# Padding rows in front of each expert's rows, written at fixed places during the attention passes

## The chip, the cores and the metric

The kernel runs on one core of a Trainium2 chip. Five engines work side by side and meet in semaphores: TensorE (PE, with its weight loads PEld), VectorE (DVE), ScalarE (ACT), GpSimd (POOL) and SyncE (SP), which here issues most of the DMA transfers. SP, ACT and POOL each have a queue of their own for DMAs (SPq, ACTq, POOLq in the profile). The metric is the device time of one execution in microseconds, lower is better.

## What is computed

The input x is 8 sequences of 512 tokens with 256 numbers each, 4096 tokens in all. First comes a layer of linear attention with a decaying sum, then a layer of experts: 32 routed experts, of which every token takes the best 4, and one shared expert. Cut to what matters:

```python
x = x + attn(layernorm(x))                    # decaying running sums of k and k*v, 8 sequences
xf = layernorm(x)
top_vals, top_idx = top_k(xf @ router_w.T + router_b, 4)
rw = softmax(top_vals) * 1.8
g = silu(einsum('th,eih->tei', xf, gate_w)); u = einsum('th,eih->tei', xf, up_w)
routed = einsum('tei,ehi,te->th', g * u, down_w, one_hot(top_idx) weighted by rw)
shared = silu(xf @ sg.T) * (xf @ su.T) @ sd.T
out = x + routed + shared
```

## The kernel before

**Two halves.** The attention runs as nine passes of a software pipeline (`steps`, b = 0 to 8), one per sequence of 512 tokens (`TS` = 4 tiles of 128) with work of two earlier sequences folded in. Pass b does the projections of sequence b ("now"), the output projection, the second norm and the router of sequence b-1 ("before"), and the numbering of the routed rows of sequence b-2 ("past"). Beside them it turns three experts' weights into place (`prep`; they come by `load_experts`, lines 365 to 369, issued by SP at the end of the pass before). Then come 192 tiles of 128 rows through the experts: 32 tiles of the shared expert (t = 0 to 31, "the shared tiles") and 160 routed tiles (t = 32 to 191). The order on each engine is the order in which the code is written.

**The lists.** A routed tile holds rows of one expert only. So every token's row (1088 bytes: its numbers in two halves, its number, its four shares and experts) is written four times into a table in HBM, `xlist`, which has a stretch of `CAP` = 4224 rows for each expert. SP loads a tile of 128 rows from `xrow` into one of four buffers `list_row` (`load_list(j)`, line 441), and POOL scatters it four times by the row numbers in `dest` (`list_rows`, line 587; 32 tiles, 128 scatters). `load_list(j)` waits until the scatters of tile j-4 have landed, since it takes their buffer, and SP stands still in that wait. 80 of the 128 scatters lie in passes 3 to 8 (twelve in each of passes 3 to 7, twenty in pass 8, woven between POOL's other work by `list_some`), 48 behind them, beside the shared tiles.

**The padding.** An expert's last tile may reach past its last row. Rows with a token number of T (= 4096) and share 0 have to stand there; their results go to a dump. Before, this padding stands behind an expert's rows, where the count of the rows puts it. The counts are known only at t = 1 (`count_tiles`, lines 952 to 957). At t = 8 to 15 SP therefore reads four places at a time (line 498) and issues four stores of 128 rows each from `pad_row` (line 500), 32 in all, with one more at line 496.

**POOL beside it.** In each pass POOL also has the products of q with the running sums (line 567 and 571, two of each), two roots for the norms (lines 576 and 578; `root(0, b+1)` for the next sequence's first norm, `root(1, b-1)` for the second norm), the split of the second norm's result in two halves (line 627), and the numbers of the rows (line 594). PE's sums over the heads (`den`, line 1276) of pass b+1 wait for both products of line 567 of pass b. VectorE's reciprocal of them (lines 838 and 840) is first in VectorE's pass.

**The shared tiles.** For a tile PE turns the rows (line 1119), multiplies by gate and up (line 1147), turns the result (1167) and multiplies by down (1180). ScalarE takes the output to `y_sb`, four buffers (line 692, or 690 for routed tiles), and SP stores it (line 493). At t = 5, 8, ... 29 the last nine experts are brought in: SP loads one (line 399), ScalarE takes its high halves (lines 700 and 702), VectorE the low ones (1037, 1039). The routed tiles can only begin behind the last of them, and their first load waits on SP for all scatters and pads (line 412).

Of the kernel before, what the change touches and what calls it, by code (L numbers as in the profile page):

```python
# [5 lines left out]
def moe_block(nc, x, w_qkv, w_out, decay_param, router_w, router_b, gate_w, up_w, down_w,  # L6
# [6 lines left out]
    P = 128  # L13
# [34 lines left out]
    with ctx:  # L48
# [12 lines left out]
        xlist = nc.dram_tensor("xlist_scratch", [E * CAP + P, ROW // 2], f32, kind="Internal").ap()  # L61
# [3 lines left out]
        x1_v = acc[0][0:T].rearrange("(b j p) h -> b p j h", j=TS, p=P)  # L65
        acc1_tiles = acc[1][0:T].rearrange("(j p) h -> j p h", p=P)
# [55 lines left out]
        pad_i = carve(E)[0:1].bitcast(i32)  # L122
        counts, tiles, tile_end = carve(E), carve(E), carve(E)
        ended = [carve(E) for _ in range(2)]
        pad_row = carve(ROW // 2)
# [45 lines left out]
        list_row = [sb(f"list_row{n}", [P, ROW // 2], f32) for n in range(LISTS)]  # L171
        payload = sb("payload", [P, TS * (ROW // 2 - H)], f32)[:, :].rearrange("p (j w) -> p j w", j=TS)
# [81 lines left out]
        counts_ready, pads_ready, pads_listed = sem("counts_ready"), sem("pads_ready"), sem("pads_listed")  # L254
# [31 lines left out]
        def tiles_listed(b):  # L286

            return range(3 * (b - 3), 3 * (b - 2)) if 3 <= b < NB else range(3 * (NB - 3), 3 * (NB - 3) + 5) if b == NB else range(0)

        IN_WINDOW = tiles_listed(NB)[-1] + 1  # L290
# [93 lines left out]
        def _(sp):  # L384
            row_at = [[sp.alloc_register(f"row_at{half}_{n}") for n in range(BATCH)] for half in range(2)]
            pad_at = [sp.alloc_register(f"pad_at{n}") for n in range(4)]
            row_of = [0] * TILES

            def rows_of(batch):

                sp.load(row_at[batch % 2], row_i[0:1, BATCH * batch:BATCH * (batch + 1)])
                for n, r in enumerate(row_at[batch % 2]):
                    row_of[NT + BATCH * batch + n] = sp.snap(r, min_val=0, max_val=E * CAP)
# [7 lines left out]
            def load_tile(t):  # L401
# [7 lines left out]
                else:  # L409
                    if t == NT:  # L410
                        for j in range(NT - LISTS, NT):
                            sp.wait_ge(*listed(j))
                        sp.wait_ge(pads_listed, 16 * (E + 1))
# [29 lines left out]
            def step(st):  # L443
                b = st.b
                if b == 3:
                    load_list(0)
                if b >= 3:
                    for j in tiles_listed(b)[1:3]:
# [17 lines left out]
                if b >= 3:  # L466
                    for j in tiles_listed(b)[3:]:
                        load_list(j)
                    load_list(tiles_listed(b)[-1] + 1)
# [10 lines left out]
            for t in range(TILES + ROUND):  # L480
# [6 lines left out]
                if t % 5 in (0, 2):  # L487
                    j = IN_WINDOW + 1 + t // 5 * 2 + (t % 5) // 2
# [5 lines left out]
                if t == 8:  # L494
# [829 lines left out]
```

## Time and profile before

| | us |
|---|---|
| median of 3 runs | 765.24 (763.4 to 765.39) |
| the profiled execution | 765.09 |
| its span, first to last instruction | 763.1 |
| PE busy | 604.8 (79%) |
| VectorE busy | 525.8 (69%) |
| ScalarE busy | 421.5 (55%) |
| POOL busy | 468.3 (61%) |

The span is 2 us shorter than the profiled execution's time, which has the start and end around it. A busy time is a sum over stages: the attention passes fill the span up to 297 us, the shared tiles from there to about 400 us, and the routed tiles what follows, with the sums of the three accumulators as the last stretch. What a change is worth has to be read in the stage where it acts.

### The profile page before, as it was taken

To read this page: it belongs to the slowest core of one execution; us is meant where nothing else is said; L and a number is where in the kernel's file an instruction comes from. 1 tells how busy PE (TensorE), PEld (TensorE's weight loads), DVE (VectorE), ACT (ScalarE), POOL (GpSimd) and SP (SyncE) were. 2 spreads that over 40 slices of the span, in tenths; PEclk is the share of its full clock that TensorE was granted. 3 is DMA by queue.
4 is the path that set the end of the run, shared out by engine and by line. 5 is a ranking of instruction groups with operands and counts; after the bars stand their busy time and mean duration, and the time that the engine had idled before them with its cause. 6 is when DMAs were issued, how large, how long until landed. Compare 5 with 4: busy or idle time off the path is not lost.

```text
span 763.1 us, 15317 instructions
## 1 busy us (share of the span) xinstructions
PE 604.8 (79%) x4649; PEld 421.6 (55%) x4649; DVE 525.8 (69%) x1931; ACT 421.5 (55%) x1008; POOL 468.3 (61%) x401
## 2 busy tenths in 40 slices
PE   4888884868768764877779999999999999999200
PEld 2455553554546453554447777777777777777100
DVE  2798996989798875664546666666666666666163
ACT  1534534352525413564557788887888887888200
POOL 3142347766666757763625778788888878888500
PEclk9998997989799876998889999999999999999755
DMA  9556264656557356999946888888988888887699
GB/s 298 201 144 187 85 189 140 197 161 207 167 159 237 102 175 196 298 328 303 310 140 123 140 141 144 142 139 138 144 144 142 145 141 136 145 140 114 127 412 395
DMA packets 122738, 140.66 MB, mean 184 GB/s; under 512 B 22370, under 2 KB 112002, under 8 KB 122626
## 3 DMA queue, kind: packets, MB, share of 16 engines
q1 hardware_dynamic: 89952, 97.42, 41.9%
q0 software_dynamic: 29184, 38.82, 30.6%
q10 hardware_dynamic: 3522, 3.44, 1.3%
q8 instruction: 39, 0.64, 0.4%
q14 instruction: 41, 0.34, 0.2%
HBM read 74.88 MB, written 65.02 MB: 183 GB/s over the span
## 4 chain that ended last, share of the span: by engine, by line
PE 52%; DVE 23%; DMA 8%; ACT 5%; SPq 4%; issue 4%; POOL 3%; POOLq 0%; ACTq 0%; DVEq 0%
PE psD L1180 12%; PE psK L1147 11%; PE psQ L1147 11%; PE psT L1119 5%; DVE W L831 2%; DMA acc_scratch<-arena 2%; SPq L509 2%; DVE arena L804 2%; DMA W<-acc_scratch 2%; DVE stats L785 2%; PE psT L1167 2%; PE psV L1167 2%; POOL xlist_scratch L587 2%; PE psT L1079 1%; PE psT L1069 1%
## 5 line engine op out<-in xcount | busy, mean ns | idle before, releaser
L650 POOL DMA_INDIRECT acc_scratch<-arena x160 | 251.4, 1571 | 78.5 <-issue 30.9
L587 POOL DMA_INDIRECT xlist_scratch<-list_row,dest x128 | 130.5, 1020 | 71.3 <-DMA list_row<-xrow_scratch 35.4
L1180 PE MATMUL psD<-W,arena 128*128 (+1 forms) x960 | 138.8, 276 | 1.0 <-DVE arena L987 0.9
L991 DVE COPY arena<-psT 128x512 f16<-128x512 f16 x192 | 81.3, 424 | 77.4 <-PE psT L1119 74.3
L1147 PE MATMUL psQ<-W,arena 128*128 (+1 forms) x576 | 113.7, 335 | 14.4 <-DVE arena L991 14.2
L1147 PE MATMUL psK<-W,arena 128*128 (+1 forms) x576 | 112.4, 333 | 12.4 <-DVE arena L991 12.2
L1180 PEld LDWEIGHTS psD<-W,arena 128*128 128x128 f16 x960 | 86.9, 99 | 8.8 <-DVE arena L987 1.1
L681 ACT ACTIVATE arena<-arena 128x192 f16<-128x192 f32 x192 | 69.6, 363 | 30.9 <-DVE arena L1015 20.0
L1147 PEld LDWEIGHTS psQ<-W,arena 128*128 128x128 f16 x576 | 51.8, 100 | 50.7 <-DVE arena L991 16.0
L1021 DVE TENSOR_TENSOR arena<-arena 128x64 f16<-128x64 f32 x192 | 43.4, 226 | 50.5 <-ACT arena L681 50.5
L1147 PEld LDWEIGHTS psK<-W,arena 128*128 128x128 f16 x576 | 51.3, 99 | 47.9 <-DVE arena L991 14.5
L1119 PE MATMUL psT<-ident,arena 128*128 128x128 f16 x768 | 76.3, 223 | 0.8 <-issue 0.7
L1119 PEld LDWEIGHTS psT<-ident,arena 128*128 128x128 f16 x768 | 58.8, 100 | 31.7 <-issue 10.3
L690 ACT ACTIVATE arena<-psD,arena 128x256 f32<-128x256 f32 x160 | 73.3, 458 | 2.2 <-DMA acc_scratch<-arena 1.4
L1022 DVE TENSOR_TENSOR arena<-arena 128x128 f16<-128x128 f32 x192 | 54.6, 285 | 0.0
L831 DVE SCALAR_TENSOR_TENSOR W<-psT,W 128x384 f16<-128x384 f32 (+1 forms) x72 | 40.1, 589 | 19.8 <-ACT W L717 19.3
L678 ACT ACTIVATE arena<-psT 128x384 f16<-128x384 f16 x96 | 47.1, 490 | 10.0 <-PE psT L1167 5.9
L721 ACT ACTIVATE W<-psK 128x512 f32<-128x512 f32 x16 | 9.6, 597 | 76.2 <-PE psK L1191 76.2
L678 ACT ACTIVATE arena<-psV 128x384 f16<-128x384 f16 x96 | 47.1, 490 | 6.5 <-PE psV L1167 1.2
L717 ACT ACTIVATE W<-psT 128x384 f16<-128x384 f32 (+1 forms) x72 | 36.4, 528 | 20.2 <-PE psT L1084 10.3
L567 POOL TENSOR_TENSOR W<-W 128x512 f32<-128x512 f32 x16 | 20.4, 1272 | 43.2 <-DVE W L815 43.1
L674 ACT ACTIVATE arena<-psQ 128x192 f32<-128x192 f32 x96 | 31.6, 330 | 26.5 <-PE psQ L1147 26.4
(156 smaller groups left out, 1115.0 us busy)
## 6 DMA issues: line engine op xcount, KB each, us to landing
arena<-xlist_scratch SPq DMA_DIRECT2D x160, 136.0 KB
W<-acc_scratch SPq DMA_DIRECT2D x24, 512.0 KB, 12.6
acc_scratch<-arena SPq DMA_DIRECT2D x16, 512.0 KB, 4.8
arena<-in_w_late_dram SPq DMA_DIRECT2D x9, 640.0 KB, 4.9
arena<-in_L_attn_x_dram SPq DMA_DIRECT2D x10, 512.0 KB, 5.4
xlist_scratch<-arena SPq DMA_DIRECT2D x33, 136.0 KB
arena<-in_L_ffn_down_w_dram SPq DMA_DIRECT2D x23, 192.0 KB
list_row<-xrow_scratch SPq DMA_DIRECT2D x32, 136.0 KB, 5.0
```

What stands on the lines that cost most here:

```text
L587: nc.gpsimd.indirect_dma_start(xlist[:, :], bass.IndirectOffsetOnAxis(ap=dest[:, n:n + 1], axis=0), list_row[j % LISTS][:, :], None).then_ ...
L650: nc.gpsimd.indirect_dma_start(acc[t % ACCS][:, :], bass.IndirectOffsetOnAxis(ap=token[:, (t - NT) % DEEP:(t - NT) % DEEP + 1], axis=0), y ...
L678: nc.scalar.activation(aT[u].rearrange("p n t -> p (n t)"), psA[u], ACT.Copy).then_inc(aT_done, 1)
L681: nc.scalar.activation(halves[t % 2][:, 0:I], act32[t % 2], ACT.Copy).then_inc(a_hi_done, 1)
L690: nc.scalar.activation(y_sb[(t - 2) % ROUND], psY[t % 2], ACT.Copy, scale=share[:, (t - 2 - NT) % DEEP:(t - 2 - NT) % DEEP + 1]).then_inc( ...
L831: nc.vector.scalar_tensor_tensor(dst, bank_of("prep", n)[:, 0:width], WS, hi, ALU.mult, ALU.subtract).then_inc(prep_lo, 1)
L991: nc.vector.tensor_copy(xT[t % 2].rearrange("p s c t -> p (s c t)"), psX[t % 2]).then_inc(xT_done, 1)
L1021: nc.vector.tensor_tensor(both[:, I:2 * P], act32[t % 2][:, P:I], both[:, P:I], ALU.subtract).then_inc(a_split, 1)
L1022: nc.vector.tensor_tensor(both[:, 2 * P:3 * P], act32[t % 2][:, 0:P], both[:, 0:P], ALU.subtract).then_inc(a_split, 1)
L1119: last = nc.tensor.transpose(psX[t % 2][:, n * P:(n + 1) * P], xg[t % XG][:, n * P:(n + 1) * P], ident16[:, :])
L1147: last = nc.tensor.matmul(psG[t % 2][:, 0:GU], xT[t % 2][:, sx, h], weights(t, (2 * h + sw) * GU, GU), start=(n == 0), stop=(n == 3 * HC - 1))
L1180: last = nc.tensor.matmul(psY[u], aT[u][0:height, part], weights(t - 2, GUW + q * H, H, height), start=(n == 0), stop=(n == len(parts) - 1))
```

## The change

1. The padding of an expert stands in front of its rows, in the first 128 rows of its stretch, at a place that needs no count. POOL makes the padding rows once, in the set-up, in `list_row[0]`; SP stores them in pass 1 into a small block in HBM, `pad_scratch`, waits for that, and copies the block from HBM to HBM to 32 fixed places: 5, 5, 6, 5, 5 and 6 copies in passes 1 to 6, behind the load of the residual and ahead of the list loads and `load_experts`. The 33 stores at t = 8 to 15 and their eight reads of places are gone.
2. The real rows of an expert begin at row 128 of its stretch: `seen[0]` starts at 1 in each of 128 partitions in place of 0, so that the ranks start at 128. The tiles of an expert are laid so that the last ends at its last row, and the first reaches back into the padding. The arithmetic of `count_tiles`, `end_tiles`, `own_tiles` and `place_tiles` on VectorE changes with it: 17 small operations in place of 16.
3. The scatters are portioned anew: 4 in pass 2 (three of them ahead of that pass's second product of line 567, one behind line 571), 14 in each of passes 3 to 7, and 20 in pass 8. That makes 94, with 34 left beside the shared tiles. In passes 3 to 8 two scatters stand ahead of the split of line 627 where one stood. The list loads on SP move with them.

```diff
+        pad_block = nc.dram_tensor("pad_scratch", [P, ROW // 2], f32, kind="Internal").ap()
...
+        pad_row = list_row[0][:, :]
...
-        def tiles_listed(b):
...
+        LIST_FROM = [0, 0, 0] + [4 + 14 * n for n in range(NB - 2)] + [94]
+        FETCHED = [(LIST_FROM[b] + 7) // K for b in range(NB + 2)]
+        PADDED = [E * max(b - 1, 0) // (NB - 2) for b in range(NB + 1)]
...
+                if j == 0:
+                    sp.wait_ge(pad_stored, 16)
...
+                if b == 1:
+                    sp.wait_ge(pads_made, 1)
+                    sp.dma_start(pad_block, pad_row).then_inc(pad_stored, 16)
+                    sp.wait_ge(pad_stored, 16)
+                if 1 <= b < NB - 1:
+                    for e in range(PADDED[b], PADDED[b + 1]):
+                        sp.dma_start(xlist_e[e, 0:P], pad_block).then_inc(pads_listed, 16)
+                if b >= 2:
+                    for j in range(FETCHED[b] + 2 if b >= 3 else 0, FETCHED[b + 1]):
                         load_list(j)
...
-                if t == 8:
-                    sp.wait_ge(pads_ready, 2)
-                    sp.dma_start(xlist[E * CAP:E * CAP + P], pad_row).then_inc(pads_listed, 16)
-                if 8 <= t < 8 + E // 4:
-                    sp.load(pad_at, pad_i[0:1, 4 * (t - 8):4 * (t - 7)])
-                    for r in pad_at:
-                        sp.dma_start(xlist[bass.ds(sp.snap(r, min_val=0, max_val=E * CAP), P)], pad_row).then_inc(pads_listed, 16)
...
-            nc.gpsimd.memset(seen[0][:, :], 0.0).then_inc(route_made, 1)
+            nc.gpsimd.memset(seen[0][:, :], 1.0).then_inc(route_made, 1)
...
-                list_some(8, 9)
+                if b >= 3:
+                    list_some(8, 10)
                 if st.before:
...
-                list_some(9, 12)
+                list_some(10 if b >= 3 else 0, 13 if b >= 3 else 3)
                 if st.now:
                     k_sum_product(b, 1)
                     kv_sum_product(b, 1)
-                list_some(12, 20)
+                list_some(13 if b >= 3 else 3, 20)
```

POOL in pass 2, from its split (line 627) to the first root of pass 3. L567 and L571 (569 and 573 in the change) are the products, L594 (596) the row numbers, L576 and L578 (578 and 580) the root. Before:

```order
L627 TENSOR_TENSOR arena<-arena 128x2x256 x2
L567 TENSOR_TENSOR W<-W 128x512
L571 TENSOR_TENSOR W<-W 128x512
L594 IOTA payload 128x4
L587 DMA xlist_scratch<-list_row,dest 135296x272 x3
L576 TENSOR_TENSOR vare<-mv,eps 128x4
L578 TENSOR_TENSOR rstd<-vare,mhalf 128x4
```

And in the changed kernel:

```order
L627 TENSOR_TENSOR arena<-arena 128x2x256 x2
L589 DMA xlist_scratch<-list_row,dest 135168x272 x3
L569 TENSOR_TENSOR W<-W 128x512
L573 TENSOR_TENSOR W<-W 128x512
L589 DMA xlist_scratch<-list_row,dest 135168x272
L596 IOTA payload 128x4
L589 DMA xlist_scratch<-list_row,dest 135168x272 x3
L578 TENSOR_TENSOR vare<-mv,eps 128x4
L580 TENSOR_TENSOR rstd<-vare,mhalf 128x4
```

The first three scatters have moved ahead of pass 2's second pair of products, and one more lies behind it.

SP at the end of pass 2, between the payload's store and the experts' loads. The change puts five copies and two list loads ahead of L365. Before:

```order
L431 DMA xrow_scratch<-payload 128x4x16
L458 DMA acc_scratch<-arena 128x4x256
L460 DMA xrow_scratch<-arena 128x4x256
L465 DMA arena<-in_L_attn_x_dram 128x4x256
L365 DMA arena<-in_L_ffn_gate_w_dram 128x3x256
```

And in the changed kernel:

```order
L430 DMA xrow_scratch<-payload 128x4x16
L457 DMA acc_scratch<-arena 128x4x256
L459 DMA xrow_scratch<-arena 128x4x256
L464 DMA arena<-in_L_attn_x_dram 128x4x256
L471 DMA xlist_scratch<-pad_scratch 16x2176 x5
L442 DMA list_row<-xrow_scratch 128x272 x2
L365 DMA arena<-in_L_ffn_gate_w_dram 128x3x256
```

Passes 1 and 3 to 6 have the copies at the same place.

## Rows read from the trace of the kernel before

**Rows 1.** Timeline of ACT, late experts' first copies: start, us, engine, line, tiles

```profile
313.58 0.83 ACT L700 ACTIVATE W<-arena 128x768 f16<-128x768 f32 x1
324.69 0.83 ACT L700 ACTIVATE W<-arena 128x768 f16<-128x768 f32 x1
...
340.52 0.83 ACT L700 ACTIVATE W<-arena 128x768 f16<-128x768 f32 x1
352.81 0.83 ACT L700 ACTIVATE W<-arena 128x768 f16<-128x768 f32 x1
...
382.15 0.83 ACT L700 ACTIVATE W<-arena 128x768 f16<-128x768 f32 x1
...
393.32 0.83 ACT L700 ACTIVATE W<-arena 128x768 f16<-128x768 f32 x1
```

**Rows 2.** Chain that ended last, 343 to 390 us: start, us, what

```profile
348.61 3.84 DMA acc_scratch<-arena
...
386.90 2.51 DMA xlist_scratch<-list_row,dest
```

**Rows 3.** Stretches: PE, PEld, DVE, ACT, POOL busy, clock, DMA share, GB/s

```profile
330.00:340.00 10.00, 8.00 (x76) 5.72 (x75) 6.11 (x19) 6.96 (x20) 6.41 (x7) 1.00 1.04 338
600.00:610.00 10.00, 10.00 (x95) 7.22 (x92) 6.83 (x37) 8.17 (x22) 8.03 (x5) 1.00 0.87 150
```

**Rows 4.** Timeline of POOL, pass 8: idle before an operation in brackets

```profile
289.15 1.03 POOL L587 DMA_INDIRECT xlist_scratch<-list_row,dest  x1 [0.20 <-issue]
290.61 2.25 POOL L627 TENSOR_TENSOR arena<-arena 128x512 f16<-128x512 f32 x2 [0.43 <-ACT arena L759]
```

**Rows 5.** Timeline of POOL, end of pass 2 and pass 3

```profile
94.96 1.27 POOL L567 TENSOR_TENSOR W<-W 128x512 f32<-128x512 f32 x1 [4.43 <-DVE W L815]
...
107.58 1.47 POOL L587 DMA_INDIRECT xlist_scratch<-list_row,dest  x1 [8.83 <-DMA list_row<-xrow_scratch]
109.35 0.97 POOL L587 DMA_INDIRECT xlist_scratch<-list_row,dest  x1 [0.30 <-issue]
...
121.49 1.04 POOL L578 TENSOR_TENSOR rstd<-vare,mhalf 128x4 f32<-128x4 f32 x1
```

**Rows 6.** Timeline of SP's queue, from pass 2's end on

```profile
95.82 1.06 SPq L365 DMA_DIRECT2D arena<-in_L_ffn_gate_w_dram  x2
...
101.93 1.99 SPq L441 DMA_DIRECT2D list_row<-xrow_scratch  x3
```

**Rows 7.** Answer for line 441 (list loads): from issue to landing

```profile
DMA to landing us min/median/max: 3.1/5.5/6.7
```

**Rows 8.** Timelines of PE and VectorE, start of pass 3

```profile
97.64 1.92 PE L1276 MATMUL psD<-W 128*128 128x8 f32 x16
...
100.11 0.20 DVE L838 TENSOR_SCALAR W<-psD 128x64 f32<-128x64 f32 x1
```

**Rows 9.** Timeline of VectorE: first sum of pass 3; the same and second norm, pass 4

```profile
106.67 0.69 DVE L811 SCALAR_TENSOR_TENSOR W<-W 128x512 f32<-128x512 f32 x1
...
145.09 0.68 DVE L811 SCALAR_TENSOR_TENSOR W<-W 128x512 f32<-128x512 f32 x1
...
157.21 2.28 DVE L804 TENSOR_SCALAR arena<-arena,mv,rstd 128x256 f32<-128x256 f32 x4
```

**Rows 10.** Answer for line 943 (row places): duration ns min/median/max

```profile
L943 DVE SCALAR_TENSOR_TENSOR dest<-payload,rank x8: 174/829/1699, 79.5 to 303.2; 128x16 int32<-128x16 f32 x8
```

**Rows 11.** Timelines of POOL and PE, pass 4: split, and who needs it

```profile
159.49 2.27 POOL L627 TENSOR_TENSOR arena<-arena 128x512 f16<-128x512 f32 x2
...
163.92 0.92 PE L1246 MATMUL psT<-ident,arena 128*128 128x128 f16 x8
```

**Rows 12.** Answer for line 475 (two copies of 128 KB, HBM to HBM): to landing

```profile
DMA to landing us min/median/max: 5.3/5.4/5.5
```

**Rows 13.** Stretches, columns as in rows 3; PE's first use of pass 4's experts

```profile
146.00:148.00 2.00, 2.00 (x11) 1.77 (x10) 2.00 (x3) 0.00 (x0) 1.43 (x1) 1.00 0.08 28
...
150.50 0.49 PE L1079 MATMUL psT<-ident,arena 128*128 128x128 f32 x3
```

More of the change, by code:

```diff
@@ L444, in step @@
                 b = st.b
-                if b == 3:
-                    load_list(0)
                 if b >= 3:
-                    for j in tiles_listed(b)[1:3]:
+                    for j in range(FETCHED[b], FETCHED[b] + 2):
                         load_list(j)
@@ L578, in root, with list_rows @@
                 nc.gpsimd.tensor_tensor(rstd[n][:, :], vare[n][:, :], mhalf[:, :], ALU.pow).then_inc(ln_rstd[n], 1)
-            def list_rows(j, which=range(K)):
-                for k in which:
-                    if k == 0:
+            def list_rows(a, z):
+                for n in range(a, z):
+                    j = n // K
+                    if n % K == 0:
                         pool.wait_ge(list_loaded[j % LISTS], 16 * (j // LISTS + 1))
                         pool.wait_ge(dest_done, j // TS + 1)
-                    n = K * j + k
                     nc.gpsimd.indirect_dma_start(xlist[:, :], bass.IndirectOffsetOnAxis(ap=dest[:, n:n + 1], axis=0),
@@ L636, in _ @@
             number_rows(NB - 1)
-            for j in range(IN_WINDOW, NT):
-                list_rows(j)
+            list_rows(LIST_FROM[NB + 1], K * NT)
             pool.wait_ge(x1_stored, 16 * NB)
@@ L969, in own_tiles @@
                 link(v.tensor_scalar(ended[n][:, :], tile_end[:, :], row[:, n:n + 1], None, ALU.is_le, ALU.add, accum_out=owner[:, n:n + 1]))
-                link(v.tensor_tensor(ended[n][:, :], ended[n][:, :], tiles[:, :], ALU.mult))
-                link(v.tensor_reduce(first[:, n:n + 1], ended[n][:, :], AX.X, ALU.add))
+                link(v.tensor_tensor(ended[n][:, 0:E - 1], ended[n][:, 0:E - 1], step_up[:, 0:E - 1], ALU.mult))
+                link(v.tensor_reduce(first[:, n:n + 1], ended[n][:, 0:E - 1], AX.X, ALU.add))
             def place_tiles():
                 v = nc.vector
-                link(v.tensor_tensor(first[:, :], row[:, :], first[:, :], ALU.subtract))
-                link(v.scalar_tensor_tensor(first[:, :], owner[:, :], float(E), first[:, :], ALU.is_lt, ALU.mult))
-                link(v.tensor_scalar(first_row[:, :], owner[:, :], float(CAP), None, ALU.mult))
-                v.scalar_tensor_tensor(first_row[:, :], first[:, :], float(P), first_row[:, :], ALU.mult, ALU.add).then_inc(owner_done, 1)
+                link(v.scalar_tensor_tensor(first[:, :], row[:, :], float(P), first[:, :], ALU.mult, ALU.add))
+                link(v.tensor_scalar(first[:, :], first[:, :], at_end[:, 0:1], None, ALU.add))
+                v.scalar_tensor_tensor(first_row[:, :], owner[:, :], float(E), first[:, :], ALU.is_lt, ALU.mult).then_inc(owner_done, 1)
             def tables_out():
```

54 lines of the change are left out of this document (26 added, 28 removed).

## The prediction

> **What bounds the kernel now.** I read the profile in three steps: the 40 slices of the page for the stages, then the chain that ended last inside each stage, then the timeline of the engines named there. The routed tiles are bound by PE alone: in a stretch of 10 us in their middle PE is busy for 10.00 us [rows 3]. The change touches nothing there. The attention passes are bound mostly by VectorE with handovers to PE, ScalarE and POOL. The shared tiles between them are the loose stage, and the pulse to read there is ScalarE's first copy of each late expert, once in three tiles [rows 1]. From 324.69 to 340.52 us two of these intervals take 15.83 us, 7.91 each, the smooth pace of three tiles. Then come 12.29 us (340.52 to 352.81), 29.34 us for three intervals to 382.15, and 11.17 us to 393.32. The chain tells what ended these waits [rows 2]: the store of an output tile, which took 3.84 us to land at 348.61 (line 493; ScalarE needs its buffer back), and at the end the last scatters of the lists, landing from 386.90 on, for which SP waits at line 412 while the last late expert's partners stand behind it. The smooth pace holds with the DMA engines at a share of 1.04 and 338 GB/s [rows 3], so full queues alone do not break it; it breaks once SP falls behind.
>
> **The shared tiles.** The change takes 33 stores of pads off SP and off the DMA engines (line 500), and eight reads of places. They stand at t = 8 to 15, so in the part where the pace breaks. It also leaves 34 scatters there in place of 48. POOL gives out one per 1.27 us (0.97 busy and 0.30 of issue [rows 5]), and before it still waited for list loads that SP issues once per two or three tiles, the last at t = 25. In the change the last list load is at t = 15. 10 scatters of pass 8 and 34 more, from 294 us on, are 44 x 1.27 = 56 us, so POOL is done near 352 us, and SP's wait at t = 26 finds everything landed. If every interval behind the first becomes 7.91 us, the stretch from 313.58 to 393.32 us (79.74 us, eight intervals) becomes 11.11 for the first, which holds the turn of the owners' table and stays, and 7 x 7.91 = 55.37, together 66.5: **13.3 us less**. That is the upper end, since 7.91 is what ScalarE, VectorE and PE need in turn. The lower end keeps the stalls behind output stores in the middle, in case it was the traffic of scatters and tile loads that made them late. Then only the first broken interval (12.29 - 7.91 = 4.4) and the last (11.17 - 7.91 = 3.3) go: 7.7 less. I take 13.3, since the pace held at DMA share 1.04, and the change adds no traffic there. What is late next is the chain ScalarE, VectorE, PE of the late experts, at 7.91.
>
> **Pass 8.** Two scatters stand ahead of the split (line 627) in place of one. Before, the one ran at 289.15 and the split began at 290.61, when ScalarE's half was just there (0.43 us of waiting) [rows 4]. A second one ends at 289.15 + 1.27 + 0.97 = 291.4, so the split begins near 291.6: **1.0 us more**, all on the path, since PE has nothing else at that point.
>
> **Passes 3 to 7.** The same extra scatter delays the split by up to 1.27 us. In pass 4 it began at 159.49 and took 2.27 us, so it ended at 161.76; 1.27 later is 163.0, and PE takes it up at 163.92 behind its turns of weights [rows 11]. Those turns hide it; with this cover gone it would cost 1.27 us in each of five passes. The other added scatter is at the end of the pass, ahead of the root for the next first norm, whose result VectorE uses only behind the second norm's statistics. I put both at 0, with 1.5 us for the five passes as the upper bound; below nothing there is no reason.
>
> **Pass 2 into pass 3.** Before, POOL waited 8.83 us at the start of pass 3 for the first list, to 107.58, because SP issued the three list loads behind the experts' loads, at 101.93 [rows 5, 6]. With the six scatters that stand ahead of the roots the second root came at 121.49 and the second norm at 122.53. The change loads two lists in pass 2, behind five pad copies and ahead of line 365, which went at 95.82 [rows 6]. I put their issue at 94. A list load lands 3.1 to 6.7 us after its issue, 5.5 in the median [rows 7]: 99.5 us. But now three scatters stand in POOL's row ahead of the second product of line 567, which began at 94.96 before [rows 5]. They take 1.77 + 1.27 + 0.97 = 4.0 us (from the starts and lengths at 107.58 and 109.35), so the product ends at 99.5 + 4.0 + 1.3 = 104.8, and not at 96.2. PE's sums over the heads wait for it: 1.92 us from 104.8 is 106.7, where they ran from 97.64 [rows 8]. VectorE's line 838 needs them and came at 100.11; it comes at 106.8, **6.7 us late**, and the whole pass 3 with it. In exchange pass 3 no longer waits for POOL. In pass 4 the second norm (157.21) comes 12.12 us behind the first sum of line 811 (145.09) [rows 9]. So in pass 3: 106.67 + 6.7 = 113.4, and 12.1 more is 125.5, against 122.53. **3.0 us more**; with the landing at 3.1 or 6.7 us it is 0.6 to 4.2. A wait is traded for another one in the pass before, and the new one is a little dearer.
>
> The stretch of pass 4 holds a hindrance by POOL. Line 943, a tiny operation, takes 174 ns at best, 829 in the median and 1699 at worst [rows 10]. The Trainium skill ("SBUF — State Buffer", "SBUF: two separate sides") says that VectorE and GpSimd share one pair of ports under an exclusive lock, held for a whole instruction, and that the other one fully blocks; the trace agrees, by that spread. By that rule pass 3 gets such a wait too, as the 12.12 us have it; without it the total would be 1.3 us lower.
>
> **The copies.** 32 copies of 139 KB from HBM to HBM stand in passes 1 to 6. Their only relatives are the two of line 475 (131 KB each), which landed after 5.3 and 5.5 us [rows 12], like a list load of the same size from its own queue. At the 338 GB/s of rows 3 one takes 0.41 us, which is the lower bound; the upper is half of 5.5, 2.75. I take 0.41, since a list load with the same landing fits in it. Six make 2.5 us. They are ahead of `load_experts`, whose loads were over at 146 to 148 us (DMA share 0.08), while PE takes the first of those experts at 150.50 [rows 13]. So some 3.5 us of slack per pass hide them. On SP they fall in the wait at line 365. In pass 1 SP also stands until the pad block has landed, some 5 us by rows 7, and issues five copies behind it; that is hidden by the same slack. POOL's two set-up operations lie in its wait for the first statistics. I put all at 0.
>
> **VectorE's tables.** 17 operations in place of 16, three of them moved: 0.2 us more, at most 0.5.
>
> **The sum.** From the profiled execution, 765.09 us (median of the runs 765.24, so nothing to correct): -13.3 + 1.0 + 3.0 + 0.2 = -9.1, **756.0 us**.
>
> **The rivals.**
> (a) *Half relieved.* The middle stalls of the shared tiles stay, because output stores land late behind scatters, which now run without gaps until 352 us. -7.7 + 4.2 = -3.5: 761.6 us. For it speaks that the chain names the landing of stores and not SP alone [rows 2], against it the smooth pace at full queues [rows 3]. 0.15.
> (b) *The trade is free.* The first list lands at 97 us, or PE's and VectorE's other work takes up the delay, and the first interval of the shared tiles shrinks as well. -13.3 + 1.2 - 1 = -13.1: 752.0 us or a little less. 0.12.
> (c) *The change gives nothing.* The scatters were never what the end waited for, and the pulse stays at 10 us because of tile loads: 765 us. Against it: the two intervals of 7.91 us, with scatters and tile loads running [rows 1]. 0.05.
> (d) *Slower.* A copy from HBM to HBM costs far more than a list load, in place of 0.41 say 1.5 us. Then 32 x 1.5 = 48 us stand ahead of the experts' loads, six passes hide 3.5 us each, 21, and 27 stay: 756 + 27 = 783 us. It decides from 3.5 / 6 = 0.6 us each. For it speaks only that just two such copies are in the trace; against it their landing in 5.5 us with eight loads ahead. 0.08.
>
> **The numbers.** The forecast (752.5 to 760) has 0.60. The range takes in (b) and most of (a): 751.0 to 762.0. Beyond 0.3% (2.3 us, about what a measurement of this kernel can tell from no change) faster: 0.60 + 0.12 + 0.13 of (a) = 0.85. Within: 0.02 of (a) and (c), 0.07. Slower: 0.08.
>
> **What the profile will show.** Line 700 at 7.9 us from the second late expert to the last, no wait at line 412, and POOL's last scatter near 352 us show the first step; an interval of 10 us or more would make (a). PE's sums of pass 3 should wait for POOL's product by some 7 us; if they do not, (b). PE's line 1079 waiting for a DMA at the start of a pass would show (d). The split of pass 8 should follow its second scatter without idle time.

## The result: slower, where faster was forecast

| | median, us | range, us | profiled execution | span | clock |
|---|---|---|---|---|---|
| before | 765.32 | 763.4 to 765.81 | 765.09 | 763.1 | 0.907 |
| changed | 774.11 | 773.22 to 774.32 | 774.22 | 772.4 | 0.899 |

The ratio is 1.0127, with a 95% interval of 1.0095 to 1.0158. The forecast was 756.0 us with a range from 751.0 to 762.0. So the time is 8.8 us longer, not 9 us shorter.

The same marks in both traces tell where it went. A "pass" here runs from VectorE's first attention product (line 852 after, 853 before) of one pass to that of the next.

| mark, us | before | after | after - before | of it new in this stretch |
|---|---|---|---|---|
| product of pass 1 | 43.03 | 42.96 | -0.1 | -0.1 |
| pass 2 | 73.91 | 72.55 | -1.4 | -1.3 |
| pass 3 | 105.48 | 111.65 | +6.2 | +7.5 |
| pass 4 | 143.89 | 151.85 | +8.0 | +1.8 |
| pass 5 | 178.05 | 187.74 | +9.7 | +1.7 |
| pass 6 | 213.03 | 225.92 | +12.9 | +3.2 |
| pass 7 | 245.42 | 257.02 | +11.6 | -1.3 |
| pass 8 | 277.44 | 292.49 | +15.1 | +3.5 |
| first late expert, ScalarE's copy | 313.58 | 330.11 | +16.5 | +1.5 |
| first routed output | 406.32 | 413.29 | +7.0 | -9.6 |
| last routed output | 712.33 | 721.98 | +9.7 | +2.7 |

The shared tiles did gain. The attention passes lost far more than that, and the prediction had given them 4 us.

**The passes.** First the timeline of POOL in the changed kernel, at the end of passes 2, 3 and 5 (start, us, engine, line; idle before it in brackets):

```profile
97.91 1.22 POOL L589 DMA_INDIRECT xlist_scratch<-list_row,dest  x1 [8.81 <-DMA list_row<-xrow_scratch]
...
101.69 1.27 POOL L569 TENSOR_TENSOR W<-W 128x512 f32<-128x512 f32 x1
...
140.60 0.96 POOL L589 DMA_INDIRECT xlist_scratch<-list_row,dest  x1 [8.20 <-DMA list_row<-xrow_scratch]
141.59 1.27 POOL L569 TENSOR_TENSOR W<-W 128x512 f32<-128x512 f32 x1
...
215.00 0.95 POOL L589 DMA_INDIRECT xlist_scratch<-list_row,dest  x1 [6.83 <-DMA list_row<-xrow_scratch]
215.97 1.28 POOL L569 TENSOR_TENSOR W<-W 128x512 f32<-128x512 f32 x1
```

POOL stands 8.81, 8.20 and 6.83 us for a list, and behind that scatter in its row is the second product of line 569 (at the end of pass 2 two more scatters stand between). Pass 7 has the same wait, 3.91 us long. Before, the product was the free one of the two [rows 5]: the wait of 8.83 us stood behind it. PE's timeline shows who pays (the same columns):

```profile
103.01 3.58 PE L1277 MATMUL psD<-W 128*128 128x8 f32 x16 [5.71 <-POOL W L569]
142.91 3.58 PE L1277 MATMUL psD<-W 128*128 128x8 f32 x16 [7.52 <-POOL W L569]
...
217.30 3.58 PE L1277 MATMUL psD<-W 128*128 128x8 f32 x16 [4.59 <-POOL W L569]
```

The sums wait 5.7, 7.5 and 4.6 us and then take 3.58 us, where the same sixteen matmuls took 1.92 [rows 8]. In all, the answer for that line says what ended PE's idle time before it, of the kernel before and then of the changed one (us, times):

```profile
  POOL W L567: 2.9, 2
```

```profile
  POOL W L569: 49.7, 10
```

Both count PE's and the weight load's waits together. The stretches of the changed kernel around pass 3's end show the second half of the price (PE, PEld, DVE, ACT, POOL busy, granted clock, DMA share, GB/s):

```profile
136.00:138.00 2.00, 0.00 (x0) 0.00 (x0) 1.38 (x15) 0.52 (x2) 0.00 (x0) 1.00 1.01 376
138.00:140.00 2.00, 0.00 (x0) 0.00 (x0) 0.00 (x0) 0.00 (x0) 0.00 (x0) 0.62 1.00 320
140.00:142.00 2.00, 0.00 (x0) 0.00 (x0) 0.00 (x0) 0.00 (x0) 1.37 (x2) 0.50 1.10 276
...
146.00:148.00 2.00, 2.00 (x5) 1.16 (x5) 1.44 (x5) 0.62 (x1) 1.56 (x2) 0.50 1.10 353
```

From 138 to 140 us no engine computes at all, and only the DMA engines are busy. TensorE's granted clock falls to 0.50, its level of 1.2 GHz, and is still there at 148 us, when PE has long been working again. A wait on POOL is paid at PE once as idle time and again as slow matmuls behind it.

**What the list waited for.** SP's queue in pass 3 (start, time of the group, line, tiles, count):

```profile
129.89 0.51 SPq L464 DMA_DIRECT2D arena<-in_L_attn_x_dram  x1
130.44 4.24 SPq L471 DMA_DIRECT2D xlist_scratch<-pad_scratch  x6
134.79 1.50 SPq L442 DMA_DIRECT2D list_row<-xrow_scratch  x2
```

Six copies hold SP's queue for 4.24 us, and the list loads come behind them. The copies cost a second thing. The load of the next sequence's x goes over ScalarE's queue; from issue to landing (min/median/max), before and then after:

```profile
DMA to landing us min/median/max: 5.0/5.2/5.7
```

```profile
DMA to landing us min/median/max: 3.9/7.5/8.8
```

Ahead of the product of pass 5 that load is on the chain that ended last: 7.92 us of transfer, then VectorE's statistics (start, us, what).

```profile
175.51 7.92 DMA arena<-in_L_attn_x_dram
...
183.46 1.41 DVE stats L784 x4
```

**The shared tiles.** ScalarE's first copies of the late experts, which answer to [rows 1]:

```profile
330.11 0.83 ACT L699 ACTIVATE W<-arena 128x768 f16<-128x768 f32 x1
339.77 0.83 ACT L699 ACTIVATE W<-arena 128x768 f16<-128x768 f32 x1
347.68 0.83 ACT L699 ACTIVATE W<-arena 128x768 f16<-128x768 f32 x1
...
363.51 0.83 ACT L699 ACTIVATE W<-arena 128x768 f16<-128x768 f32 x1
373.08 0.83 ACT L699 ACTIVATE W<-arena 128x768 f16<-128x768 f32 x1
...
400.14 0.83 ACT L699 ACTIVATE W<-arena 128x768 f16<-128x768 f32 x1
```

No interval is over 10 us any more. Four are 7.91 us, and the other four are 9.6 to 9.7. The waits for a store of a tile and at line 412 [rows 2] are gone. What makes a 9.57 is on PE's timeline; its first row belongs to an interval of 7.91, the others to two of 9.57 and 9.58:

```profile
351.02 1.15 PE L1148 MATMUL psQ<-W,arena 128*128 128x384 f16 x6 [2.00 <-DVE arena L992]
...
366.84 1.82 PE L1148 MATMUL psQ<-W,arena 128*128 128x384 f16 x6 [2.00 <-DVE arena L992]
...
379.20 1.94 PE L1148 MATMUL psQ<-W,arena 128*128 128x384 f16 x6
```

and in the stretches (columns as above):

```profile
352.00:354.00 2.00, 2.00 (x22) 1.49 (x20) 1.23 (x5) 1.45 (x4) 1.39 (x3) 1.00 0.87 231
...
364.00:366.00 2.00, 0.84 (x11) 0.52 (x8) 1.11 (x2) 1.46 (x4) 1.56 (x2) 1.00 0.99 366
366.00:368.00 2.00, 1.16 (x5) 0.67 (x6) 1.48 (x5) 0.64 (x2) 0.68 (x1) 0.79 0.44 124
368.00:370.00 2.00, 2.00 (x14) 1.51 (x12) 0.69 (x2) 0.88 (x3) 0.00 (x0) 0.50 0.94 329
```

PE idles for 2.00 us while VectorE finishes a late expert ahead of line 992 (366.84), and then the granted clock is 0.50 for the next few us, with groups of 1.8 to 1.9 us in place of 1.14. But the wait alone doesn't decide it. In the intervals of 7.91 us PE waits just as long (1.81 to 2.00 us, as ahead of 351.02), and there the clock stays at 1.00. So the same wait is followed by a slow clock at some late experts and not at others; what picks them was not found. The first interval, 9.66 us, is another matter: the clock stayed at 1.00 in it.

### The profile page after: what moved, and what is told of

The parts are those of the page before. It is cut to its first block, busy times and chain, and to the rows that moved or that the text cites. A ratio compares the mean times of both kernels' runs of the same rounds, so it can differ in the third digit from the quotient of the medians.

```text
span 772.4 us, 15244 instructions
## 1 busy us (share of the span) xinstructions
PE 611.7 (79%) x4649; PEld 428.2 (55%) x4649; DVE 516.5 (67%) x1932; ACT 420.9 (54%) x1008; POOL 464.4 (60%) x401
## 4 chain that ended last, share of the span: by engine, by line
PE 55%; DVE 18%; issue 9%; POOL 7%; DMA 4%; ACT 4%; SPq 2%; POOLq 0%; ACTq 0%; DVEq 0%
PE psD L1181 12%; PE psK L1148 12%; PE psQ L1148 12%; PE psT L1120 6%; POOL xlist_scratch L589 4%; SPq L507 2%; PE psD L1277 2%; DMA W<-acc_scratch 2%; PE psT L1168 2%; PE psV L1168 2%; DVE stats L784 2%; PE psQ L1192 2%; POOL arena L627 1%; DVE W L830 1%; PE psD L1221 1%
## 5 line engine op out<-in xcount | busy, mean ns | idle before, releaser
L649 POOL DMA_INDIRECT acc_scratch<-arena x160 | 248.7, 1554 | 110.9 <-DMA acc_scratch<-arena 61.6
L1148 PE MATMUL psK<-W,arena 128*128 (+1 forms) x576 | 112.0, 332 | 10.9 <-DVE arena L992 10.8
L1148 PE MATMUL psQ<-W,arena 128*128 (+1 forms) x576 | 112.2, 332 | 10.3 <-DVE arena L992 10.2
L673 ACT ACTIVATE arena<-psK 128x192 f32<-128x192 f32 x96 | 31.6, 330 | 25.6 <-PE psK L1148 25.3
```

The costliest lines, as they stand in the source:

```text
L649: nc.gpsimd.indirect_dma_start(acc[t % ACCS][:, :], bass.IndirectOffsetOnAxis(ap=token[:, (t - NT) % DEEP:(t - NT) % DEEP + 1], axis=0), y ...
L673: nc.scalar.activation(gate, psG[t % 2][:, 0:I], ACT.Silu, scale=1 / WS).then_inc(silu_done, 1)
L1148: last = nc.tensor.matmul(psG[t % 2][:, 0:GU], xT[t % 2][:, sx, h], weights(t, (2 * h + sw) * GU, GU), start=(n == 0), stop=(n == 3 * HC - 1))
```

## The experiments

Three suspicions came out of this. **List:** the portions of 14 place a fresh list ahead of the second product. **Copies:** they hold SP's queue and lengthen x's load. **Clock:** PE's idle time behind VectorE costs twice. Ten kernels were run. They came in three groups, each timed beside the kernel before, whose medians there were 764.42, 764.40 and 765.13 us. In the table, "passes" is from the first attention product of pass 1 to that of pass 8, "tiles" from the first late expert to the first routed output, "x" the median landing of x's load over ScalarE's queue. The three stages are from one profiled execution each, and executions of one kernel differ (the kernel before ran from 758.2 to 767.2 us in the second group), so a stage's difference of 2 us is no more than a hint, and one of 5 us is more.

| kernel | median | ratio, 95% interval | passes | tiles | x |
|---|---|---|---|---|---|
| before | 765.32 | | 234.4 | 92.7 | 5.2 |
| changed | 774.11 | 1.0095 to 1.0158 | 249.5 | 83.2 | 7.5 |
| pads only | 764.11 | 0.9981 to 1.0066 | 237.9 | 84.8 | 5.3 |
| portions only | 769.69 | 1.0046 to 1.0107 | 238.3 | 88.1 | 5.9 |
| products first | 762.83 | 0.9963 to 1.0011 | 239.2 | 83.3 | 6.8 |
| lists ahead of copies | 763.84 | 0.9956 to 1.0015 | 243.9 | 83.3 | 7.7 |
| both orders | 759.91 | 0.9899 to 1.0000 | 237.7 | 83.2 | 5.3 |
| copies in the tiles | 764.54 | 0.9976 to 1.0021 | 236.3 | 87.6 | 5.4 |
| copies behind experts | 761.95 | 0.9936 to 0.9976 | 237.8 | 83.3 | 5.2 |
| in the tiles, PE kept busy | 758.71 | 0.9908 to 0.9951 | 236.6 | 84.5 | 5.3 |
| all three | 755.59 | 0.9844 to 0.9902 | 237.0 | 76.7 | 5.4 |
| before, PE kept busy | 766.26 | 0.9981 to 1.0031 | 233.1 | 91.3 | 5.2 |

(The expectations put down 239.0 for the passes of "products first"; the trace has 239.2.)

### 1. The pads alone

The copies, the set-up and the tables of the change, with the old portions and list loads (one of the edited places):

```
-        LIST_FROM = [0, 0, 0] + [4 + 14 * n for n in range(NB - 2)] + [94]
+        LIST_FROM = [0, 0, 0] + [12 * n for n in range(NB - 2)] + [80]
```

> The new padding alone; the scatters and list loads are portioned as before (12 in passes 3 to 7, 20 in pass 8, one ahead of the split, list loads at their old places). Theory A (the loss is the wait for a freshly loaded list ahead of the second product on POOL, in passes 2, 3, 5 and 7 of the changed kernel): those waits are gone, PE's sums over the heads wait for no product, pass 3 is as long as before, and the shared tiles keep their gain from the pads that left. 757 to 761 us, faster than before by 4 to 8. Theory B (the loss is the traffic and SP time of the 32 copies from HBM to HBM, which lengthen the loads of x, of the lists and of the experts): the passes stay as long as in the changed kernel, 770 us or more.

764.11 us, no difference from before that can be measured, and in neither theory's range (three of its ten runs took over 770 us). Theory A's first part holds: PE's sums wait for POOL's product no more than before (2.9 us in all, two times). The passes take 3.5 us more than before, and the tiles take 8.0 less. VectorE now waits for x's load (waits by releaser: us in total, times, longest):

```profile
DVE stats L786 <- DMA arena<-in_L_attn_x_dram: 12.2, 5, 5.2
```

The kernel before had 5.6 us in three such waits. So the copies are hardly free, but alone they are far from the 16.5 us.

### 2. The portions alone

The kernel before with the scatters and list loads of the change; the pads stay stores at the shared tiles. One of the edited places:

```
-                if b == 3:
-                    load_list(0)
                 if b >= 3:
-                    for j in tiles_listed(b)[1:3]:
+                    for j in range(FETCHED[b], FETCHED[b] + 2):
                         load_list(j)
```

> The new portions of scatters and list loads alone; the padding stays as in the kernel before (33 stores at t = 8 to 15). Theory A: the waits ahead of the second product come back in passes 2, 3, 5 and 7, each shorter by the 3.6 to 4.2 us which the copies took on SP's queue: some 6 to 9 us more in the passes, with only the last wait of the shared tiles gone (3.3 us): 769 to 772 us. Theory B: without copies the passes are as before, 762 us.

769.69 us, in theory A's range. The passes take 3.9 us more than before, under the 6 to 9 expected (the profiled execution was 3.5 us under the median of the runs). 3.5 and 3.9 make 7.4, and together they cost 15.1, but the medians do not show so big a rest (-0.3 and +5.3 make 5.0, and the change costs 8.8), so its size is open. That the two meet is plain in the waits. The same answer as above, PE's and the weight load's idle time for POOL's product, has 2.9 us before, 2.9 with the pads alone, 34.5 here and 49.7 with both. POOL's waits for a list ahead of the product are 6.06, 4.49, 4.34 and 3.70 us here and 8.81, 8.20, 6.83 and 3.91 with both: the copies stand in SP's queue in front of just those list loads that the new portions need ahead of the product.

### 3. The second products ahead of the scatters

```
-                list_some(10 if b >= 3 else 0, 13 if b >= 3 else 3)
                 if st.now:
                     k_sum_product(b, 1)
                     kv_sum_product(b, 1)
-                list_some(13 if b >= 3 else 3, 20)
+                list_some(10 if b >= 3 else 0, 20)
```

> The changed kernel with one edit on POOL: the scatters that stood ahead of the second products of a pass (three in every pass from 2 to 7) come behind them. Theory A: PE's sums over the heads wait for no list any more and run at full clock; 12 to 13 us of the passes come back: 760 to 763 us. Theory B: nothing changes on the side of the traffic, so the loads of x still land late and the time stays above 770 us.

762.83 us, 11.3 less than the changed kernel, in theory A's range. PE's idle time for POOL's product is back at 2.9 us, from 49.7, and the passes fall by 10.3 us. POOL's timeline at the end of pass 3 shows it:

```profile
131.24 1.27 POOL L569 TENSOR_TENSOR W<-W 128x512 f32<-128x512 f32 x1 [3.37 <-DVE W L813]
...
138.80 0.95 POOL L589 DMA_INDIRECT xlist_scratch<-list_row,dest  x1 [1.43 <-DMA list_row<-xrow_scratch]
```

The product starts at 131.24 in place of 141.59 us, as soon as VectorE's result is there. The list's wait is still there, 1.43 us of it, but nobody stands behind it. Nothing is given up for it: three scatters go behind two products of 1.27 us, and nobody needs them soon. Of the 4.8 us that the passes still take over those before, VectorE's waits for x can be a part: 14.5 us in five, where the kernel before had 5.6 in three.

### 4. The list loads ahead of the copies

```
-                if 1 <= b < NB - 1:
-                    for e in range(PADDED[b], PADDED[b + 1]):
-                        sp.dma_start(xlist_e[e, 0:P], pad_block)...
                 if b >= 2:
                     for j in ...:
                         load_list(j)
+                if 1 <= b < NB - 1:
+                    for e in range(PADDED[b], PADDED[b + 1]):
+                        sp.dma_start(xlist_e[e, 0:P], pad_block)...
```

> The changed kernel with one edit on SP: the list loads of a pass come ahead of the pad copies. Theory A: a list lands 3 to 4.2 us earlier, so each of the four waits shrinks by that: 762 to 765 us. Theory B: the same copies are there, only in another order: 772 to 775 us.

763.84 us, 10.3 less than the changed kernel. SP's queue and POOL in pass 3:

```profile
128.31 1.54 SPq L442 DMA_DIRECT2D list_row<-xrow_scratch  x2
129.90 4.12 SPq L474 DMA_DIRECT2D xlist_scratch<-pad_scratch  x6
```

```profile
134.93 0.96 POOL L589 DMA_INDIRECT xlist_scratch<-list_row,dest  x1 [5.26 <-DMA list_row<-xrow_scratch]
```

The wait ahead of the product shrinks to 5.26 us and does not vanish, and the passes keep 243.9 us. Even a list that is first in SP's queue behind the residual comes too late for a product that could start at 131 us. The copies are only a part of the delay. PE's idle time for POOL's product is 26.6 us here, against 49.7 and 2.9. By the medians (763.84 and 762.83) the two orders can't be told apart. (The profiled execution of this kernel was 5 us over the median of its runs, so its passes are rather too long.)

### 5. Both orders

> The changed kernel with two orders altered and all work kept: GpSimd does both second products of a pass ahead of the scatters that stood before them, and SyncE issues the list loads of a pass ahead of its copies. Each of these alone brought the changed kernel from 774 us to 763 or 764 us. Theory A (one wait, for a fresh list ahead of the second product, which either order removes): both together bring hardly more than one, 760 to 764 us, and passes 2 to 8 take about 237 us from the first attention product to the last, as with either alone (239.0 and 243.9; 234.4 in the kernel before). Theory B (two separate losses, GpSimd's own wait and the backlog in SyncE's queue): the gains add up, 751 to 754 us. In both theories the x loads stay near 7 us or over, since the copies are still beside them.

759.91 us, just under theory A's range and 6 us over theory B's: mostly one loss, which either order removes. The part on x's load missed. It landed after 5.3 us in the median, not 7, though the copies still stood beside it, and the worst was 8.4.

### 6. The copies at the shared tiles

"Products first", and the copies moved:

```
+                if 8 <= t < 8 + E // 4:
+                    if t == 8:
+                        sp.wait_ge(pad_stored, 16)
+                    for e in range(4 * (t - 8), 4 * (t - 7)):
+                        sp.dma_start(xlist_e[e, 0:P], pad_block)...
```

> The changed kernel with the second products ahead of the scatters (as in the run 'products first') and the 32 copies taken out of the passes: SyncE issues them from the one block of pads, four per tile, at shared tiles 8 to 15, where the kernel before wrote its pads. All work is kept, the scatter's portions of 14 too. Theory A (the copies cost the passes their x loads, which landed in 6.8 us median beside them and in 5.2 before): passes fall by 3.5 to 5 us against 239.0, the x load's median returns to 5.2 to 5.5 us, the list loads on SyncE start at once; shared tiles as in the changed kernel or 1 us more: 757 to 760 us. Theory B (the copies themselves cost nothing and the longer x loads come from the two more scatters of a pass): passes stay at 239, x loads stay at 6.5 to 7 us, 762 to 764 us.

x lands after 5.4 us, as theory A expects, and the passes go its way but not as far: 236.3 in place of 239.2 us, 2.9 less where 3.5 to 5 were expected. The time is 764.54 us, outside both ranges, since the tiles take 87.6 in place of 83.3. The chain that ended last names how (start, us, what; L496 is a copy):

```profile
335.47 0.49 SPq L496
...
337.29 0.59 SPq L496
337.92 4.95 DMA acc_scratch<-arena
...
343.24 0.83 ACT W L699
```

Four copies hold SP for 2.4 us, and only then comes the store of a tile (line 499), which lands 4.95 us later, and ScalarE needs its buffer before it goes on. This is the stall of the kernel before [rows 2]. It needs no reading of places and no stores from a buffer: four copies of 136 KB on SP ahead of the tile's store make it too.

### 7. The copies behind the experts' loads

"Products first", and the pass's copies issued on SP behind `load_experts`.

> The changed kernel with the second products ahead of the scatters, and the pass's 5 or 6 copies issued on SyncE behind the pass's experts' loads in place of ahead of its last list loads. All work is kept. If what the copies cost is their place (they stand in front of list loads and beside the x load of the pass): passes at 235 to 237 us in place of 239.0 and 758 to 761 us. If it is their 3.6 to 4.2 us of SyncE's queue or their traffic wherever it stands: the next pass's first list loads and residual stores start later by about 4 us, passes stay at 239 or longer, 762 to 765 us.

761.95 us and passes at 237.8 us, each just outside the first theory's range. The same 32 copies, still in the passes, with the same bytes, but x lands after 5.2 us in the median and 5.6 at worst, where "products first" had 6.8 and 8.5, and VectorE's waits for it are 6.0 us in place of 14.5. So for x it is the copies' place that counts. What that is worth in time is small: 1.5 us of passes (239.2 to 237.8) and 0.9 of the medians, no more than a hint. The ratio to before, 0.9936 to 0.9976, is the first of the runs up to here whose whole interval is below one.

### 8. PE kept busy

"Copies in the tiles", and behind every late expert PE repeats ten matmuls of the tile before, into a bank that the tile's own first matmul overwrites:

```
+                    if t >= 1 and late_tile(t - 1) is not None:
+                        for r in range(10):
+                            nc.tensor.matmul(psG[t % 2][:, 0:GU], xT[(t - 1) % 2][:, 0, r % HC],
+                                             weights(t - 1, 2 * (r % HC) * GU, GU), start=(r == 0), stop=(r == 9))
                     pe.wait_ge(xT_done, t + 1)
```

> As the run with the copies at the shared tiles, and in addition TensorE repeats ten matmuls of the tile before (128x384, into the bank that the tile's own first matmul then overwrites) while it waits for VectorE behind each late expert. It tests why three shared tiles take 9.6 us in half of the cases where 7.9 was forecast. Theory C (TensorE stands idle for 2.0 us behind VectorE's work on the late expert, the granted clock falls to 0.50 for the next 3 to 4 us, and the groups of L1148 take 1.8 to 1.9 in place of 1.14 us): with TensorE kept busy the clock stays at 1.0 and every interval is 7.9 to 8.2 us; six or so intervals of 9.6 give back 1.7 us each, 6 to 10 us less than its twin. Theory D (the time is VectorE's or the DMAs', the clock only follows): intervals of 9.6 us stay, time as its twin within 1 us, or later by the repeated matmuls.

758.71 us, 5.8 less than its twin. From the sixth late expert on the intervals are 7.9, 7.9 and 8.0 us, where the twin has 7.9, 9.6 and 9.7. That is theory C's mechanism; the size is just short of its 6 to 10 us, and the two intervals give 3.3 us in the traces. The three intervals beside the copies keep their stalls (9.2, 12.1 and 10.3 us): they are there with PE kept busy as well, so repeated matmuls do not remove them.

### 9. All three

"Copies behind experts" with PE kept busy.

> The changed kernel with the three things that the runs so far point to, and no work left out: both second products ahead of the scatters, the pass's copies behind its experts' loads, and TensorE repeating ten matmuls while VectorE finishes a late expert. If the terms are separate, this is the run with the copies behind the experts' loads (761.95 us) less 1.7 us for each of its five intervals of 9.6 or 9.7 us: 752 to 756 us, every interval of the late experts 7.9 to 8.2 us. If the gain of the clock is given back behind the late experts (a stage behind them that starts no earlier), the first routed output stays 83 us behind the first late expert and the time is 760 to 762 us.

755.59 us, at 0.9873 of the kernel before (0.9844 to 0.9902), faster than both kernels and in the range for separate terms (though "copies behind experts" has four slow intervals in its trace, and not five). Seven intervals are 7.9 or 8.0 us:

```profile
316.82 0.83 ACT L699 ACTIVATE W<-arena 128x768 f16<-128x768 f32 x1
326.48 0.83 ACT L699 ACTIVATE W<-arena 128x768 f16<-128x768 f32 x1
...
382.01 0.83 ACT L699 ACTIVATE W<-arena 128x768 f16<-128x768 f32 x1
...
393.54 0.46 ACT L689 ACTIVATE arena<-psD,arena 128x256 f32<-128x256 f32 x1
```

and PE's idle time behind VectorE is 0.38 us, with the clock at 1.00 behind it, as in the whole stage from 316 to 394 us (shown for one late expert):

```profile
361.53 1.15 PE L1152 MATMUL psK<-W,arena 128*128 128x384 f16 x6 [0.38 <-DVE arena L992]
```

```profile
362.00:364.00 2.00, 2.00 (x21) 1.46 (x19) 1.11 (x4) 1.57 (x6) 0.00 (x0) 1.00 0.89 246
```

### 10. The kernel before with PE kept busy

> The kernel before with TensorE repeating the same ten matmuls behind each late expert, and nothing else altered. It prices the share of the shared tiles that is TensorE's clock alone in the kernel before. In its trace five of eight intervals are over 10 us (11.1, 12.3, 10.8, 10.6, 11.2) and they stand on waits for late expert loads and stores as well. If the clock's part is 1.7 us each as in the changed kernel: 8 us less in all, about 757 us. If the intervals are held by transfers beside POOL's scatters, and the clock only follows them: 763 to 766 us. The combined kernel sent beside this one then shows what the fixed places of the pads are worth over it.

766.26 us, no difference from before (0.9981 to 1.0031). Two of its intervals stay at 13.5 and 10.9 us and the last at 11.1: they are held by the store of a tile and by the last scatters. So what makes the combined kernel faster is the change's own relief of the shared tiles and the clock together, and the clock alone gives nothing that can be measured. This run shows one thing more: the routed tiles, from the first to the last output, take 308.5 us here.

## Why the prediction was wrong, step by step

- **Passes 3 to 7, put at 0: this step failed.** It asked only whether the extra scatters delay the split and the root, by their own 1.27 us. It did not ask which scatter of a pass is the first of a list. With portions of 14, in passes 3, 5 and 7 the last scatter ahead of the second product is the first of a fresh one, and POOL stands there for 8.20, 6.83 and 3.91 us with PE's sums behind. At VectorE's second norm of pass 3 the changed kernel was 1.1 us behind (123.70 against 122.64); at the product of pass 8 it was 15.1. That is 14 us of passes where 0 was put; the waits for POOL and the late x (next point) both lie in it, and were not told apart within it. Run 3 alters nothing but POOL's order, ends PE's waits for the product and brings the time back by 11.3 us, and so shows the cause.
- **The copies, put at 0.** The slack ahead of the experts' first use did hide the copies' bytes, and PE's line 1080 never waited for a transfer, so rival (d) did not come about. Two other users of the time were missed. The list loads stand behind the copies on SP (4.24 us for six), and the next x's load lands 2.3 us later in the median. Alone this costs 3.5 us of passes in one trace (run 1), and nothing that the medians can tell.
- **Pass 2 into pass 3, +3.0: the mechanism was right, the sum was +1.1.** The list came at 97.9 (99.5 forecast) and PE's sums waited 5.7 us. VectorE's line 837 came 6.5 us late, where 6.7 was forecast for it as line 838, and line 810 started at 112.85 (113.4). That it fits so well is partly luck: the slow matmuls behind the wait, 3.58 and 3.76 us in place of 1.92 and 1.96, were not in the sum, and the earlier list made up for them. The later half, that pass 3 regains time since its own first wait is gone, was true too and was put too small: the second norm came 10.85 us behind line 810, not 12.1. The gain was overtaken by the new wait at 140.60. Even without that wait it did not last: in "products first" pass 3 takes 33.5 us where it took 38.4 before, and pass 4 takes 38.9 where it took 34.2.
- **The hindrance by POOL, expected in pass 3: absent.** Line 942 took 0.17 us there at 117.20, the undisturbed time of [rows 10]. POOL ran a product of line 569 until 116.68 and began a scatter at 116.85. So line 942 fell beside other work, and the 12.12 us of pass 4 were no measure for it; the 1.3 us that the prediction priced it at is just what came off. In the kernel before, line 943 took 1.44 to 1.70 us in passes 4 to 7, where in passes 4 to 6 POOL's product began 0.12 us behind it, and 0.17 to 0.22 in the other four, where no product ran beside it. The Trainium skill ("SBUF — State Buffer", "SBUF: two separate sides"), which the prediction leant on, states an exclusive lock for a whole instruction; these rows agree, and what failed was where the two would meet.
- **Pass 8, +1.0: right.** POOL's timeline has the second scatter and the split directly behind it, without idle time; 1.5 us were lost from pass 8's product to the first late expert.

```profile
305.58 0.96 POOL L589 DMA_INDIRECT xlist_scratch<-list_row,dest  x1 [0.30 <-issue]
306.56 2.27 POOL L627 TENSOR_TENSOR arena<-arena 128x512 f16<-128x512 f32 x2
```

- **The shared tiles, -13.3: right in kind, over-sized.** The eight intervals went from 79.74 to 70.03 us, 9.7 less. The first was 9.66 and not 11.11 (1.4 better). Three of the other seven took 9.6 us and not 7.91 (5.0 worse). The smooth pace of [rows 1] is the pace at full clock; it was read from intervals that had PE's 2.00 us of idle time behind VectorE as well, but kept the clock, and the sum took all seven to be of that kind. In run 9, with 0.38 us of idle time, all seven are. POOL's last scatter ended at 366.7 us and not near 352, since the stage began 16.5 us late. Rival (a) had named the stores of tiles. They were not it: their waits were gone.
- **The routed tiles, put at 0, took 308.7 us, 2.7 more.** The change was not shown to be at fault: the other kernels take 307.1 to 309.4 us, and the kernel before with PE kept busy 308.5, with the same code there. The 306.0 us of the kernel before were rather a good execution; what makes the difference was not found.

The rivals: (a) to (c) all took the passes as known to within 4 us, and (d), the one on the slower side, priced the copies' bytes. None was about the order on POOL in the passes behind the first. The added chance of "slower", 0.08, was too small: a change that re-portions work of one engine among fixed neighbours can move a wait in front of another engine's operand in any pass. The prediction worked this out for pass 2, where the wait was plain, and did not repeat the count for the passes behind it.

What stays open: how the copies lengthen x's load, which is on another queue. In the five kernels with the copies ahead of the experts' loads the slowest x load took 8.4 to 8.8 us (8.8, 8.8, 8.5, 8.5, 8.4); in the kernel before, with PE kept busy or not, and in the four kernels with the copies behind the experts' loads or out of the passes it took at most 5.9. But "portions only" has no copies in the passes and one x load of 9.8 us, so the copies are not the only thing that makes it late. Order among the transfers and reads of the same memory were not told apart. Open too is why the clock falls behind some late experts and not behind others, with the same idle time of PE. Also open are the 2.6 us that the passes of the best kernel still take over those of before.

## What to carry to other kernels

When an engine's side work is cut in other portions, write down for each portion which item needs a fresh transfer, and which work of that engine, needed elsewhere, comes behind it; do so for every pass and not only for the first. Put what others wait for ahead of what nobody waits for: here the reordering cost nothing and brought the changed kernel back to the time of the kernel before. A transfer that is "hidden" should be weighed by the queue time of its issue too, and by what is issued behind it: here the same copies, issued behind the experts' loads, no longer made x late.

## What the runs showed of the hardware that was not expected

- An idle PE can be paid twice. After 2.00 us of waiting for VectorE the granted clock was 0.50 (1.2 GHz) in the stretch behind four of the nine late experts of the changed kernel, and in the three of these that open an interval 1.7 us were lost on top (9.6 in place of 7.91 us); behind the other five, with 1.81 to 2.02 us of waiting, it stayed at 1.00. With PE's wait of 7.52 us for POOL it fell to 0.50 and was still there at 148 us, and the sixteen matmuls of the sums took 3.58 in place of 1.92 us. With ten matmuls repeated in the gap it stayed at 1.00 from 316 to 394 us (run 9), and in run 8 they gave 5.8 us.
- A copy of 136 KB from HBM to HBM holds the issuing queue for 589 ns in the median (529 to 1063), a list load of the same size from HBM into SBUF for 426 (320 to 1377). In a row six took 4.24 us.
- With the copies ahead of the experts' loads, a transfer on another queue landed late: the slowest x load took 8.4 to 8.8 us in each of five kernels, against 5.7 before. The median went from 5.2 to 7.5 in the changed kernel, but stayed at 5.3 in two of the five. In the changed kernel the DMA share was 1.00 to 1.14 from 136 to 148 us.
